# A two-layer transformer block on one core: score matmuls on 64-row halves of TensorE, and long pieces divided among the half steps

## The reference

```python
x = x + attn0(layernorm(x), wq, bq, wk, bk, wv, bv, wo, bo)      # 16 heads of 8 channels
x = x + ffn0(layernorm(x), w_gate, w_up, w_down)                 # int weights / 127, silu(gate) * up, hidden 384
x = x + attn1(layernorm(x), Wqkv, bqkv, Wproj, bproj, qn_w, kn_w)  # q and k are rms-normed per head
x = x + moe1(layernorm(x), base_w, base_b, lora_A, lora_B, router_w, router_b)

scores = softmax(einsum('bhse,bhte->bhst', q, k) / sqrt(8))      # both attentions, 512 x 512 a head
att    = einsum('bhst,bhte->bhse', scores, v)
```

## Time and profile before

| | |
|---|---|
| median of three runs | 2164.41 us (2163.48 to 2167.84) |
| the profiled execution | span 2165.0 us, mean granted clock 0.957 of 2.4 GHz |
| PE busy | 1980.4 us, 91% |
| DVE busy | 1638.9 us, 76% |
| ACT busy | 1431.8 us, 66% |
| POOL busy | 434.7 us, 20% |
| DMA | 140.94 MB, mean 65 GB/s |
| score matmuls | 4096, two forms of 2048 |
| value matmuls | 4096 instructions, 8 in a group |
| maxima on DVE | 2048, 1323.5 us |

### The profile page before, as it was taken

The page is one execution under the profiler, slowest core; times in us unless marked ns, Lnnn a source line. Parts: engine busy times, 40 slices in busy tenths (PEclk is TensorE's granted clock), DMA queues, the critical chain, the costliest instruction groups (busy, mean ns, idle before and its releaser), DMA issues.

```text
span 2165.0 us, 38228 instructions
## 1 busy us (share of the span) xinstructions
PE 1980.4 (91%) x10706; PEld 763.2 (35%) x10706; DVE 1638.9 (76%) x3602; ACT 1431.8 (66%) x2921; POOL 434.7 (20%) x571
## 2 busy tenths in 40 slices
PE   3958999999999999999999999999999999999785
PEld 1223333333333333333333333333333333333332
DVE  5638888787887878778787877878787778888471
ACT  2615676676766767676776767677676767676643
POOL 2112121131212113121211312121121213121200
PEclk8858999999999999999999999999999999999977
DMA  5112314040311404031130404114050412302020
GB/s 108 55 25 58 87 34 122 18 135 19 111 44 39 116 17 137 17 116 39 46 109 17 138 16 119 36 46 109 17 138 17 118 36 62 94 20 72 18 63 16
DMA packets 162656, 140.94 MB, mean 65 GB/s; under 512 B 38761, under 2 KB 144050, under 8 KB 162482
## 3 DMA queue, kind: packets, MB, share of 16 engines
q1 hardware_dynamic: 162482, 139.29, 23.2%
HBM read 77.38 MB, written 55.57 MB: 61 GB/s over the span
## 4 chain that ended last, share of the span: by engine, by line
PE 62%; issue 15%; DVE 10%; DMA 5%; POOL 4%; ACT 2%; SPq 2%; DVEq 0%; POOLq 0%; ACTq 0%
PE ps L1159 17%; PE ps L1134 14%; PE ps L1144 14%; DVE neg_max L881 5%; PE ps L1209 4%; PE ps L1110 3%; PE ps L1173 3%; PE ps L1182 2%; PE ps L1214 2%; DMA k_stack<-k_rows 2%; ACT probs L661 1%; DVE bn L858 1%; DMA k_rows<-kp 1%; PE ps L1221 1%; DMA rden_all<-rden_rows 1%
## 5 line engine op out<-in xcount | busy, mean ns | idle before, releaser
L881 DVE TENSOR_REDUCE neg_max<-ps 128x1 f32<-128x512 f32 x2048 | 1323.5, 681 | 231.2 <-PE ps L1134 194.0
L661 ACT ACTIVATE probs<-ps 128x512 f32<-128x512 f32 x2048 | 1093.8, 599 | 347.2 <-PE ps L1144 345.6
L1134 PE MATMUL ps<-k_stack,q_stack 96*128 96x512 bf16 x2048 | 798.7, 392 | 80.2 <-DVE neg_max L881 51.2
L1144 PE MATMUL ps<-q_stack,k_stack 128*128 128x512 bf16 x2048 | 782.7, 385 | 16.8 <-ACT probs L661 14.0
L1159 PE MATMUL ps<-probs,v_aug 128*32 128x512 f32 x4096 | 548.8, 608 | 0.4
L1144 PEld LDWEIGHTS ps<-q_stack,k_stack 128*128 128x128 bf16 x2048 | 202.9, 100 | 441.8 <-ACT probs L661 244.9
L1134 PEld LDWEIGHTS ps<-k_stack,q_stack 96*128 96x128 bf16 x2048 | 202.3, 99 | 371.7 <-DVE neg_max L881 192.4
L561 POOL TENSOR_TENSOR o_raw<-o_raw,rden_all 128x512 f32<-128x512 f32 x64 | 81.4, 1272 | 580.7 <-DMA rden_all<-rden_rows 580.7
L1159 PEld LDWEIGHTS ps<-probs,v_aug 128*32 128x32 f32 x4096 | 80.7, 108 | 184.4 <-ACT probs L661 102.3
L667 ACT ACTIVATE xn<-x,shift,rstd 128x128 f32<-128x128 f32 x192 | 80.7, 486 | 49.4 <-POOL shift L544 49.3
L578 POOL TENSOR_TENSOR ht<-up,gs 128x512 f32<-128x512 f32 x48 | 60.9, 1268 | 257.3 <-ACT up L642 257.3
(11 more groups left out here) (109 smaller groups left out, 1487.5 us busy)
## 6 DMA issues: line engine op xcount, KB each, us to landing
q_stack<-q_rows SPq DMA_DIRECT2D x128, 192.0 KB, 3.4
k_stack<-k_rows SPq DMA_DIRECT2D x128, 192.0 KB, 4.3
rden_all<-rden_rows SPq DMA_DIRECT2D x64, 256.0 KB
q_rows<-qp SPq DMA_DIRECT2D x32, 384.0 KB, 2.6
k_rows<-kp SPq DMA_DIRECT2D x32, 384.0 KB, 3.0
q_rows<-qp SPq DMA_DIRECT2D x32, 256.0 KB, 2.9
k_rows<-kp SPq DMA_DIRECT2D x32, 256.0 KB, 3.0
x_in<-in_L_attn_x SPq DMA_DIRECT2D x16, 256.0 KB, 2.8
```

The lines of the kernel that those rows point to most:

```text
L661: act.activation(probs[:, u % RING, :], ps[:, bank_of(l, u), :], ACT.Exp).then_inc(exps, 1)
L881: dve.tensor_reduce(neg_max[l][:, pair // 2, col:col + 1], ps[:, BANKS + bank_of(l, n), :], AX.X, ALU.max, negate=True).then_inc(max_taken, 1)
L1134: pe.matmul(ps[:, BANKS + bank_of(l, 2 * n + e), :], q_stack[l][0:QROWS, pair, tok:tok + 128], k_stack[l][e][0:QROWS, pair, :], start=True ...
L1144: pe.matmul(ps[:, bank_of(l, u), :], k_stack[l][e][:, pair, tok:tok + 128], q_stack[l][:, pair, :], start=True, stop=True).then_inc(scores, 1)
```

## The change

The second copy of k goes. `k_stack[l]` and `q_stack[l]` now hold the first head of a pair in rows 0 to 47 and the second in rows 64 to 111, the rows of maxima and ones behind each (48, 49 and 112, 113). A `max_score` reads the 48 rows of one head, an `attend_score` the 50 rows; where the attend score of an h is on one half, its max score is on the other (e is turned round, and DVE's column with it). The ones are set by two memsets of POOL at the start, which fill all of `k_stack` with ones; nothing is cleared. `max_rows` becomes two DMAs, one for each half.

PE's loop goes over the 64 half steps, and most pieces are divided into parts. Part k of a piece with n parts at step s goes into sub-slot 4s + (3, 1, 0 for n = 1, 2, 4) + (4/n)k; sub-slots 2h and 2h+1 are served behind half step h, and behind its `attend_pv` if it has one. So a piece of one part stays behind h = 2s+1, one of two parts has its first behind h = 2s and its second behind 2s+1, and one of four has two behind each. What a piece waits for it waits for ahead of part 0. DVE's `project_add`, statistics and moments of pr0 and pr1, `down_add` and what follows are moved by one half step.

```diff
+PARTS_OF = {"q0": 2, "k0": 2, "v0": 2, "v1": 2, "rt": 2, "pr0": 4, "pr1": 4, "dn": 4, "out": 4, "qka": 2, "qkb": 2,
+            "g0": 2, "u0": 2, "g1": 2, "u1": 2, "g2": 2, "u2": 2}
+def sub_slots(name, at_step):
+    n = PARTS_OF[name] if name in PARTS_OF else 1
+    first = {1: 3, 2: 1, 4: 0}[n]
+    return [(4 * at_step + first + (4 // n) * k, k, k == n - 1) for k in range(n)]
...
-                sp.dma_start(q_stack[l][QROWS:QROWS + 2 * MROWS, 2 * quarter:2 * quarter + 2, :],
-                             m_parts[l][quarter % 2][:, :]).then_inc(m_in[l][quarter], 16)
+                for e in (0, 1):
+                    sp.dma_start(q_stack[l][HALF * e + KROWS:HALF * e + AROWS, 2 * quarter:2 * quarter + 2, :],
+                                 m_parts[l][quarter % 2][16 * e:16 * e + 16, :]).then_inc(m_in[l][quarter], 16)
...
             pool.memset(mid_bias[:, EXPERTS:], 0.0)
+            for l in (0, 1):
+                pool.memset(k_stack[l][:, :, :].rearrange("p a b -> p (a b)").bitcast(F32), ONE_PAIR).then_inc(k_ones, 1)
...
-                    zero_stacks((*k_stack[0], q_stack[0]))
                     place_weights()
-                    set_ones(0)
...
-                            if h == 19:
+                            if h == 20:
                                 project_add(0, x1, i)
-                            if h == 20:
+                            if h == 21:
                                 dve.wait_ge(read["pr0"], i + 1)
                                 stats(1, x1, i)
-                            if h == 21:
+                            if h == 22:
                                 moments(1, i)
                                 factors_in(1, i)
                             if at == 0 and h == 23:
                                 clear_values(1)
-                                dve.wait_ge(k_zeros, 3)
-                                set_ones(1)
...
-                pe.matmul(ps[:, BANKS + bank_of(l, 2 * n + e), :], q_stack[l][0:QROWS, pair, tok:tok + 128],
-                          k_stack[l][e][0:QROWS, pair, :], start=True, stop=True).then_inc(max_scores, 1)
+                n, e = m // 2, 1 - m % 2
...
+                tok, pair, row = 128 * (n % 4), n // 4, HALF * e
+                pe.matmul(ps[:, BANKS + bank_of(l, m), :], q_stack[l][row:row + KROWS, pair, tok:tok + 128],
+                          k_stack[l][row:row + KROWS, pair, :], start=True, stop=True).then_inc(max_scores, 1)
...
-                pe.matmul(ps[:, bank_of(l, u), :], k_stack[l][e][:, pair, tok:tok + 128],
-                          q_stack[l][:, pair, :], start=True, stop=True).then_inc(scores, 1)
+                tok, pair, row = 128 * kt, 2 * group + pp, HALF * e
+                pe.matmul(ps[:, bank_of(l, u), :], k_stack[l][row:row + AROWS, pair, tok:tok + 128],
+                          q_stack[l][row:row + AROWS, pair, :], start=True, stop=True).then_inc(scores, 1)
...
                 elif name[0] in "gu":
-                    pe.wait_ge(read["xt1"], b + 1)
+                    if k == 0:
+                        pe.wait_ge(read["xt1"], b + 1)
                     w = w_gate if name[0] == "g" else w_up
-                    last = pe.matmul(gen, w[:, int(name[1]), :], xnt[1][:, :], start=True, stop=True)
+                    last = by_column(w[:, int(name[1]), :], xnt[1], k)
...
+                plan = {q: (name, k, last) for at_step, name in pieces for q, k, last in sub_slots(name, at_step)}
+                for h in range(2 * STEPS):
...
+                    if "A" in have:
+                        attend_score(now[0], h, now[1])
+                    if mx:
+                        max_score(*mx)
...
+                    if h % 4 == 3 and h > 3 and "A" in have:
+                        attend_pv(now[0], h - 7, now[1])
+                    for q in (2 * h, 2 * h + 1):
+                        if q in plan:
+                            name, k, last = plan[q]
+                            op = piece(name, k, i, at, kind, i + PIECE[name][0])
+                            if last:
+                                op.then_inc(written[sem_name(name)], 1)
```

More of the change, by code:

```diff
@@ L423, in stack_half @@
                     hold(scores, UNITS * attends_before(l, b - 1) + 32 * (half + 1))
-                for rows, stacks in ((q_rows[l], (q_stack[l], q_stack[l])), (k_rows[l], k_stack[l])):
+                for rows, stack in ((q_rows[l], q_stack[l]), (k_rows[l], k_stack[l])):
                     for e in (0, 1):
@@ L427, in stack_half @@
                                       [[SEQ, KROWS], [HD * TERMS * SEQ, 4], [1, SEQ]])
-                        sp.dma_start(stacks[e][KROWS * e:KROWS * e + KROWS, 4 * half:4 * half + 4, :], src
+                        sp.dma_start(stack[HALF * e:HALF * e + KROWS, 4 * half:4 * half + 4, :], src
                                      ).then_inc(stack_in[l][half], 16)
@@ L471, in slot @@
                     if at == 1:
[L472 removed]
+                        hold(k_ones, 2)
                     if "M2" in have:
@@ L810, in _ @@
         def _(dve):
[L811 to L817, removed]
-                k0, k1 = (t[:, :, :].rearrange("p a b -> p (a b)") for t in k_stack[l])
-                dve.memset(k0[QROWS:QROWS + MROWS, :], 1.0).then_inc(k_ones, 1)
-                dve.memset(k1[QROWS:QROWS + 2 * MROWS, :], 1.0).then_inc(k_both, 1)
-                dve.wait_ge(k_both, l + 1)
-                dve.memset(k1[QROWS:QROWS + MROWS, :], 0.0).then_inc(k_ones, 1)
             def clear_values(l):
@@ L1168, in turn_norm, with by_token @@
                 return last
-            def by_token(dst, xt, w, more=None):
-                for t in range(TT):
+            def by_token(dst, xt, w, tiles, more=None):
+                for t in tiles:
                     last = pe.matmul(dst[:, t, :], xt[:, 128 * t:128 * t + 128], w, start=True, stop=more is None)
@@ L1176, in by_token, with by_column, project, piece @@
                 return last
-            def project(l, b):
-                pe.wait_ge(att_ready[l], 2 * b + 2)
-                for t in range(TT):
-                    for c in (0, 1):
-                        last = pe.matmul(gen4[:, t, :], o_raw[l][:, c, 128 * t:128 * t + 128], wo[l][:, c, :],
-                                         start=c == 0, stop=c == 1)
+            def by_column(w, xt, half):
+                return pe.matmul(gen[:, 256 * half:256 * half + 256], w, xt[:, 256 * half:256 * half + 256],
+                                 start=True, stop=True)
+            def project(l, t):
+                for c in (0, 1):
+                    last = pe.matmul(gen4[:, t, :], o_raw[l][:, c, 128 * t:128 * t + 128], wo[l][:, c, :],
+                                     start=c == 0, stop=c == 1)
                 return last
-            def piece(name, i, at, kind, b):
+            def piece(name, k, i, at, kind, b):
                 before = piece_before(kind, at, name)
-                if before is not None:
+                if k == 0 and before is not None:
                     pe.wait_ge(read[sem_name(before[0])], count(before[0], i + before[1]))
@@ L1192, in piece @@
                 elif name in ("q0", "k0"):
-                    pe.wait_ge(read["xt0"], b + 1)
-                    last = pe.matmul(gen, (wq if name == "q0" else wk)[:, :], xnt[0][:, :], start=True, stop=True)
+                    if k == 0:
+                        pe.wait_ge(read["xt0"], b + 1)
+                    last = by_column((wq if name == "q0" else wk)[:, :], xnt[0], k)
                 elif name == "v0":
-                    pe.wait_ge(read["xt0"], b + 1)
-                    last = by_token(gen4, xnt[0], wv[:, :])
+                    if k == 0:
+                        pe.wait_ge(read["xt0"], b + 1)
+                    last = by_token(gen4, xnt[0], wv[:, :], (2 * k, 2 * k + 1))
                 elif name == "v1":
-                    last = by_token(gen4, xnt[2], wqkv[:, 256:384])
+                    last = by_token(gen4, xnt[2], wqkv[:, 256:384], (2 * k, 2 * k + 1))
                 elif name[0] == "m":
@@ L1235, in piece @@
                 elif name == "out":
-                    last = by_token(gen4, xnt[3], w_base[:, :], more=(coef_t, w_lora[:, :]))
-                last.then_inc(written[sem_name(name)], 1)
+                    last = by_token(gen4, xnt[3], w_base[:, :], (k,), more=(coef_t, w_lora[:, :]))
+                return last
             def slot(kind, i, at):
@@ L1249, in slot @@
                             pe.wait_ge(read["k0"], 1)
-                            last = by_token(gen4, xnt[0], wv[:, :])
+                            last = by_token(gen4, xnt[0], wv[:, :], range(TT))
                         else:
```

94 lines of the change are left out of this document (40 added, 54 removed).

## The result

The changed kernel takes 2441.9 us (median of 4 runs, 2427.3 to 2449.2) against 2165.5 us before: ratio 1.1264, interval [1.1226, 1.1303]. The forecast was 2231 us, range 2060 to 2345. Slower was right; the size was missed by 211 us, and the range with it. The profiled run has a span of 2425.4 us.

What follows compares the result with a forecast made beforehand. TensorE was nearest its limit (91% busy), bounding the g/u stretch, with VectorE pacing elsewhere. Fifteen Y slots at +8.0, fifteen X at -2.4 and once -18.2 gave +66 us on 2165.0: 2231 us, range 2060 to 2345.

Steps and rivals of the forecast that it cites:

- Y sum of +8.0: Y slot: earlier waits of divided pieces and later VectorE work add 8.0 us a slot, bounds -4 to +12.
- rival (d): TensorE's clock could fall to 1.2 GHz in Y with waits there: +8 us a slot, 2350 us; chance 0.05.
- The step of pr0: Y slot: pr0's wait now stands at h=18, half of pr0 follows it, and h=20 comes 1.0 us later.
- The g/u cycle: Y slot: g to u +1.05 us, three times, and u to g +0.28, twice; together +3.7 us.
- X: X slot: stack load 2.0 us earlier, 26 steps behind it -0.4; -2.4 us a slot, bounds -6 and +1.
- Once: Start and end of the run: earlier stack loads -6.7 us, Y0 -5.5, X0 and Y16 -3 each; together -18.2.
- Score pairs starting less than 0.05 us apart: Sign in the changed profile that the two scores of a half step run together on different halves.
- Rival (b): The halves don't run together, so a half step still costs 0.43 us: 2350 us; chance 0.06.
- (c): Rival: weight loads wait for their half of the rows, 0.10 us a half step: 2290 us; chance 0.04.
- Rival (a): Freed TensorE time covers the waits, X -5 and Y -4 us a slot: 2012 us; chance 0.22.
- The later additions of VectorE: Y slot: project_add and what follows one half step later cost +0.9 us, down_add to xt2 +0.6.
- drain at a change of tiling mode: Skill's rule: changing tiling mode drains the engine; at 0.24 us a round trip for every part, some 30 us more.

Runs made afterwards that it cites:

- e5: The changed kernel with score matmuls issued again ahead of the Y pieces that wait: 2362.3 us, 1.0919 of the kernel before.
- e1: The change with undivided pieces and project_add and down_add at their old half steps: 2128.4 us, 0.9811 of the kernel before.
- e6: As e1, but both scores of a half step on the same half of the rows: 2143.6 us, 0.9896 of the kernel before.
- e7: As e1, but VectorE's project_add and down_add one half step later: 2170.8 us, 1.0014 of the kernel before.
- e11: As e1, but with the X pieces (q0, k0, v1, rt, pr1, out) divided: 2150.4 us, 0.9936 of the kernel before.
- e10: The changed kernel with dn, qka and qkb undivided, all else the same: 2407.2 us, 1.1121 of the kernel before.
- e8: The changed kernel with pr0 and pr1 undivided, all else the same: 2368.0 us, 1.0944 of the kernel before.
- e2: The changed kernel with scores on the whole array and two k copies, as before; pieces still divided: 2372.4 us, 1.0936 of the kernel before.
- e9: The changed kernel, pieces divided, but both scores of a half step on the same half of the rows: 2598.0 us, 1.2017 of the kernel before.
- run 80: Not a run label: 80 us is how much faster e5 ran than the changed kernel; e5 measured 2362.3 us.

## Why the prediction was wrong

The failed step is the clock. The Y sum of +8.0 prices every piece at 2.4 GHz, and rival (d), "With waits in Y it could fall to 1.2 GHz there", stood beside it as a separate case with a chance of 0.05. It belonged inside the sum: the forecast itself put waits into Y. The earlier trace rows already showed a stretch with waits at 0.58. The size that (d) gave it, +8 us a slot, was near what it came to. The step of pr0 shows it best: the walk has 1.0 + 0.25 + 1.1 + 1.0 = 3.35 us from pr0's start to h=20; it took 3.49 at the full clock and 6.07 at the low one. Over the twelve Y slots of after, the length follows 74.8 us + 0.31 us for each us of low clock (correlation 0.97); e5, with other low times, gives 74.8 + 0.32. So of the 17.6 us that a Y slot gained, 7.3 are clock and 10.3 are there at full clock. The split leans on that line; in the other kernels with much low clock in Y its slope is 0.27 to 0.39.

Where the 194 us between forecast and profiled execution (2425.4 against 2231) went:
- Clock in Y: 14 slots x 7.3 = 102 us.
- Y at full clock: +10.3, forecast +8.0: 14 x 2.3 = 32 us. The g/u cycle took 6.39 to 6.42 us where my walk gives 3.97 + 2.10 = 6.07. A part with its crossing took 0.63 us (1258.79 to 1259.42) for my 0.55, and an h between two parts 0.32 for 0.25. Three turns make 1.0 of the 2.3. For pr0 I had a gain of 0.3 to 0.4 us in the normalisation; it came 13.76 us into the slot for 13.84 before, 0.1 earlier.
- X: the fifteen slots X1 to X15 were shorter by 5.3 us together (-0.6 in the loop) where the forecast has 15 x 2.4 = 36: 31 us. The stack load still ends the wait: M38 now waits 2.04 us for k_stack instead of 0.85. The max rows were issued 1.65 us earlier in the slot (30.13 for 31.78), but the second of their DMAs stands behind them, and M38 came 1.15 us earlier for the forecast's 2.0. The 26 half steps behind it took 22.83 us for 22.85, where I had -0.4.
- Once: the first exponential came 4.8 us earlier (forecast 6.7), X0 with Y0 0.8 (8.5), Y16 0.3 (3.0): 12 us. Y15 with X16 took 125.4 us for 104.0, where the forecast has +8.0: 13 us. The low clock in them rose from 34.1 to 65.3 us; if the 0.31 of the Y slots holds there, that is 9.7 us of it.

These come to 190 of 194; the rest is that Y1 and Y14, outside the mean of the twelve, grew by 39.2 us together and not by 35.2.

Point by point (where the forecast says "steps" in its walk, as in "4.73 us for four", it counts half steps, and the waits of rows 3 are those of X8 with the Y slot before it; no sum hangs on either):
- "Score pairs starting less than 0.05 us apart": right (0.00 to 0.01 where neither waits), and the next pair follows 0.22 us later (1248.13 to 1248.35). Rival (b) is refuted. So is (c): the max score of one h and the attend of the next share a half and are not held up. The Trainium skill (TensorE: Matmul & The Clock Gate, Part 3: Packing small matmuls) has the load overlap only in another row group; no pair here shows such a wait. In the trace of after a load for the next attend score starts at 1387.04, beside the max score of 1387.03 on the same half.
- "u.0 about 1.55 us after the end of g.1, PE idle for 1.3": right, 1.48 us and 1.09.
- "DVE idle in Y up from 12 to about 20": 24.7 us (76.84 - 52.11) in the faster slot, 32 in the slower.
- "Y near 71": wrong. "X near 60": right by the level (60.2 and 61.6), though the gain was smaller.
- "PE's busy time well down": wrong. 1980 became 1989. The saving is real, for in the X slot with clock 1.00 it fell from 58.95 to 51.23 us; in Y the matmuls at 1.2 GHz took it back (61.81 before, 63.59 and 71.93 after).
- "First stack loads at 34 to 35": right, 35.13.
- Rival (a), freed PE time covering the waits: refuted in Y, where a turn of g and u took 6.4 us and not 4.73 or less; e1 shows the halves with their start to be worth 39 us when no wait is moved, and e6 the running together 15 of them.
- The later additions of VectorE: +1.5 a slot forecast, +3.3 measured, of which 1.0 to 1.7 at full clock (e7).

Of the drain at a change of tiling mode (the Trainium skill, TensorEngine Tiling (Array Packing), Key Properties) the forecast said some 30 us more. The parts of the X slots in e11 made the slot 0.11 us longer each, less than the 0.24 of the value group. In the g and u stretch of Y a part takes 0.63 - 0.43 = 0.20 us over the forecast's array time, and the h ahead of the next part 0.32 (1258.47 to 1258.79) where a pair costs 0.22: 0.30 for the round trip, an estimate. So the 0.24 is too high for what X loses and somewhat low where nothing hides the crossing; whether the engine drains at each change no run here separates from other overhead.

Open: why the low clock is at times 13.7 and at times 37.5 us in slots with the same instructions, why in e10 it moved into X, and what part of the low clock in Y comes of the rows and what of the longer idle time ahead of pr0. e8, on halves with a wait at pr0 about as long as e2's, comes nearest; e2 with a wait as long as e9's would tell more, and was not run.

## What to carry to other kernels

Dividing a piece and placing its first part earlier moves the wait of the whole piece earlier too; where the reader of one piece feeds the next, each latency must be covered again by what is left between them, so count that cover before dividing. When a change adds waits to TensorE or makes its matmuls use fewer rows, put the granted clock into the sum itself, not among the accidents: here the division on the whole array and the halves without division each left the clock at full speed in Y, and both together took some 7 us of each slot. Try the two halves of a combined change apart: one was worth -39 us and was buried under the other.

## What the runs showed of the hardware

- Two matmuls on different 64-row halves start within 0.01 us of each other and take the time of one (0.39 us, the next pair 0.22 us later).
- Two kernels with the same parts and the same number of score matmuls had a granted clock of 1.00 and 0.79 in a Y slot, the one with 96 to 128 rows and the other with 48 to 50 (e2, e9). Ahead of pr0 TensorE idled for 1.24 us in the one and 2.35 in the other, so the rows are not shown to be the cause.
- In the five kernels whose TensorE idles for 1.8 to 3.3 us ahead of pr0, the clock fell to 1.2 GHz 13 to 17 us into 55 of 60 Y slots; in the nine where it idles there for 1.5 us or less, into 4 of 108.
- Sixty redundant matmuls in the waits of a slot made it 6 us shorter on average, and the run 80 us (e5).
- Going from scores on halves to a piece on the whole array and back made X slots 0.11 us a part longer (e11) and took 0.30 us in the g/u stretch of Y, an estimate from 0.63 and 0.32 us against 0.43 and 0.22.
